# Feed-forward Gelus in two groups of four, with four result slots and later consumers

## The reference

```python
x = x + attention(layernorm(x))
P = layernorm(x) @ U1
H = gelu(P @ V1 + b1, approximate=True)
x = x + (H @ U2) @ V2 + b2
```

## Time and profile before

| what | value |
|---|---|
| runs | 3236.54, 3237.70, 3242.32 us; median 3237.7 us |
| the profiled execution | 3231.01 us; its span 3229.2 us |
| mean granted TensorE clock | 0.972 of full speed |
| busy: PE, DVE, ACT, POOL | 89%, 79%, 75%, 54% of the span |
| Gelus | 128, 81.4 us in all |
| ACT table loads | 61 at the Gelu, 60 at the exponential, 1 at the start |

### The profile page before, as it was taken

The page is one execution under the profiler, slowest core; times in us unless marked ns, Lnnn a source line. Parts: engine busy times, 40 slices in busy tenths (PEclk is TensorE's granted clock), DMA queues, the critical chain, the costliest instruction groups (busy, mean ns, idle before and its releaser), DMA issues.

```text
span 3229.2 us, 98431 instructions
## 1 busy us (share of the span) xinstructions
PE 2884.6 (89%) x32328; PEld 1994.1 (62%) x32328; DVE 2555.6 (79%) x7419; ACT 2422.1 (75%) x4212; POOL 1731.4 (54%) x1560
## 2 busy tenths in 40 slices
PE   4899898998989899898998989989898998989986
PEld 1566565665657666575665656656575665656664
DVE  6888787887878878787787878868788787878863
ACT  3677877777787777787877787777877777777784
POOL 1455555555555555555555555555555555555564
PEclk9999999999999999999999999999999999999998
DMA  4010010100101011010110101001010111101000
GB/s 131 22 34 21 25 33 18 41 20 24 34 18 41 19 30 28 23 36 18 35 26 23 34 17 41 20 24 34 18 42 19 31 26 24 36 16 42 19 19 8
DMA packets 66472, 94.33 MB, mean 29 GB/s; under 512 B 11019, under 2 KB 39691, under 8 KB 65675
## 3 DMA queue, kind: packets, MB, share of 16 engines
q1 hardware_dynamic: 65940, 87.53, 10.9%
HBM read 27.73 MB, written 8.39 MB: 11 GB/s over the span
## 4 chain that ended last, share of the span: by engine, by line
PE 29%; issue 28%; POOL 26%; DVE 6%; ACT 5%; POOLq 1%; DVEq 0%; ACTq 0%
POOL p_lo L1055 24%; PE proj L418 13%; PE scores L418 6%; PE o_acc L418 5%; PE ffn_acc L418 2%; PE max_scores L418 2%; DVE max_scores L902 1%; DVE q_hi_lo L825 1%; ACT L716 1%; ACT h_f L798 1%; DVE v_lo L825 1%; PE transposes L545 1%; ACT p_f L716 1%; ACT L798 1%; POOL h_lo L1078 1%
## 5 line engine op out<-in xcount | busy, mean ns | idle before, releaser
L1055 POOL TENSOR_TENSOR p_lo<-p_f,p_hi 128x512 f16<-128x512 f32 x1280 | 1476.7, 1157 | 1171.7 <-ACT p_hi L674 1140.1
L716 ACT ACTIVATE p_f<-scores 128x512 f32<-128x512 f32 x1280 | 757.7, 592 | 319.5 <-PE scores L418 309.4
L674 ACT ACTIVATE p_hi<-p_f 128x512 f16<-128x512 f32 x1280 | 800.0, 625 | 49.3 <-issue 33.0
L902 DVE CUSTOM_DVE_ANT_0 max_scores<-max_scores,causal 128x384 f32<-128x384 f32 (+3 forms) x1184 | 564.1, 508 | 198.5 <-PE max_scores L418 191.6
L418 PE MATMUL scores<-q_hi_lo,k_lo_hi 128*128 128x512 f16 (+3 forms) x2048 | 622.5, 304 | 28.8 <-issue 27.7
L418 PE MATMUL scores<-q_hi_aug,k_hi_aug 128*128 128x512 f16 (+3 forms) x2048 | 596.7, 304 | 0.0
L418 PE MATMUL o_acc<-v_hi_one,p_lo 128*128 128x65 f16 x5120 | 527.2, 196 | 46.6 <-POOL p_lo L1055 46.5
L418 PEld LDWEIGHTS o_acc<-v_hi_one,p_lo 128*128 128x128 f16 x5120 | 477.1, 99 | 83.7 <-issue 44.8
L418 PE MATMUL o_acc<-v_hi_one,p_hi 128*128 128x65 f16 x5120 | 527.7, 195 | 0.0
L418 PE MATMUL o_acc<-v_lo,p_hi 128*128 128x64 f16 x5120 | 527.5, 194 | 0.0
L418 PEld LDWEIGHTS o_acc<-v_lo,p_hi 128*128 128x128 f16 x5120 | 474.1, 99 | 19.5
(11 more groups left out here) (110 smaller groups left out, 5644.2 us busy)
## 6 DMA issues: line engine op xcount, KB each, us to landing
q_hi_lo<-q_hi_aug SPq DMA_DIRECT2D x256, 128.0 KB, 2.2
k_lo_hi<-k_hi_aug SPq DMA_DIRECT2D x128, 128.0 KB, 2.2
x_rows<-in_L_attn_inputs SPq DMA_DIRECT2D x17, 512.0 KB, 4.5
x_residual<-in_L_attn_inputs SPq DMA_DIRECT2D x16, 512.0 KB, 4.3
out<-x_rows SPq DMA_DIRECT2D x16, 512.0 KB, 4.2
k_hi_aug<-in_k_aug SPq DMA_DIRECT2D x128, 20.0 KB
q_hi_lo<-in_L_attn_W_qkv SPq DMA_DIRECT2D x1, 2048.0 KB, 10.4
q_hi_aug<-in_L_attn_W_qkv SPq DMA_DIRECT2D x1, 2048.0 KB, 15.0
```

The costliest lines, as they stand in the source:

```text
L674: return nc.scalar.activation(out_ap, in_ap, ACT.Copy, scale=scale)
L716: nc.scalar.activation(p_f[:, k % 3, :], score_bank[k % 2][:, :], ACT.Exp).then_inc(exp_done, 1)
L902: last = nc.vector.tensor_tensor_reduce(out=bank, in0=bank, in1=causal[:, (T - 1 - qt) * P:S], scale=1.0, scalar=-3e38, op0=ALU.add, op1=A ...
L1055: nc.gpsimd.tensor_tensor(p_lo[:, slot, n, :], p_f[:, k % 3, :], p_hi[:, slot, n, :], ALU.subtract).then_inc(lo_p, 1)
```

## The change

FFN_PAIRS, until now one table for four engines, is split: FFN_PAIRS is only `ffn_h` on PE, GELU_AT the Gelus on ACT (chunks 0 to 3 at (13, 1), 4 to 7 at (14, 2)), H_PAIRS the cast on DVE and the low part on POOL, U2_PAIRS `ffn_u2` on PE. `h_f32` has four slots instead of two, so Gelu c waits for `h_lo` of chunk c-4 and no more of c-2. `h_hi` and `h_lo` keep two slots. The copy and low part of `ffn_acc` (QF_AT) move from (15, 1) to (15, 2). No operation is added or left out.

```diff
-FFN_PAIRS = {(13, 1): 0, (13, 3): 1, (14, 0): 2, (14, 2): 3}
-
-U2_PAIRS = {(13, 4): 0, (14, 0): 1, (14, 2): 2, (14, 4): 3}
+FFN_PAIRS = {(13, 1): 0, (13, 2): 1, (14, 2): 2, (14, 3): 3}
+
+GELU_AT = {(13, 1): range(0, 4), (14, 2): range(4, 8)}
+
+H_PAIRS = {(13, 2): 0, (13, 4): 1, (14, 3): 2, (15, 0): 3}
+
+U2_PAIRS = {(13, 4): 0, (14, 1): 1, (14, 4): 2, (15, 1): 3}
 U2_START = 13 * SEG + 4
 
-QF_AT, Y_AT = (15, 1), (15, 4)
+QF_AT, Y_AT = (15, 2), (15, 4)
...
-        h_f = sb("h_f32", [P, 2, S], F32)
+        h_f = sb("h_f32", [P, 4, S], F32)
...
-                            if (s, n) in FFN_PAIRS:
-                                for c in (2 * FFN_PAIRS[s, n], 2 * FFN_PAIRS[s, n] + 1):
+                            if (s, n) in GELU_AT:
+                                for c in GELU_AT[s, n]:
                                     act.wait_ge(pe_h, at((i - 1) * FC + c + 1 + FREE))
 
-                                    act.wait_ge(lo_h, at((i - 1) * FC + max(c - 1, 0) + FREE))
-                                    nc.scalar.activation(h_f[:, c % 2, :], proj("h", c)[:, :], ACT.Gelu_apprx_tanh,
+                                    act.wait_ge(lo_h, at((i - 1) * FC + max(c - 3, 0) + FREE))
+                                    nc.scalar.activation(h_f[:, c % 4, :], proj("h", c)[:, :], ACT.Gelu_apprx_tanh,
...
-                            if (s, n) in FFN_PAIRS:
-                                pair = FFN_PAIRS[s, n]
+                            if (s, n) in H_PAIRS:
+                                pair = H_PAIRS[s, n]
...
-                                    nc.vector.tensor_copy(h_hi[:, c % 2, :], h_f[:, c % 2, :]).then_inc(hi_h, 1)
+                                    nc.vector.tensor_copy(h_hi[:, c % 2, :], h_f[:, c % 4, :]).then_inc(hi_h, 1)
...
-                            if (s, n) in FFN_PAIRS:
-                                pair = FFN_PAIRS[s, n]
+                            if (s, n) in H_PAIRS:
+                                pair = H_PAIRS[s, n]
...
-                                    nc.gpsimd.tensor_tensor(h_lo[:, c % 2, :], h_f[:, c % 2, :], h_hi[:, c % 2, :],
+                                    nc.gpsimd.tensor_tensor(h_lo[:, c % 2, :], h_f[:, c % 4, :], h_hi[:, c % 2, :],
```

## The result

The changed kernel takes 3285.9 us (median of four, 3285.09 to 3292.24), the kernel before, run beside it, 3237.1: ratio 1.016, interval 1.014 to 1.018. It is slower by 1.6%; forecast were 3283 us and slower. Its profiled execution has a span of 3290.4 us against 3229.2, so the two profiles differ by 61 us, 12 more than the medians (the profiled execution before is one of the shorter ones, that after the longest of its four), and a stage by 4.0 us.

What follows compares the result with a forecast made beforehand. No engine full: a chain through four in-order engines, PE nearest to full at 89%. 15 stages x 2.9 us plus 1.9 in LAST gave +45.4, from 3231.0 to 3276.4, plus 6.7 to the median: 3283 us, range 3200 to 3312.

Steps and rivals of the forecast that it cites:

- The loads: ACT, MID stages: 4 loads fewer a stage, 5.13 us each stage, 77 us over 15; 31 at Gelu, 30 at exponential.
- The first group: Gelus 0 to 3 at (13, 1): ACT idles 0.97 before Gelu 2; exponential (13, 2) comes 2.1 us later.
- Attend (14, 1): PE at (14, 1): attend waits 1.35 us for POOL's last p_lo, as casts and POOL ops take turns.
- The 1.5 us at the maxima of (14, 0): PE, ahead of attend (14, 1): a wait of 1.5 us for the maxima of (14, 0).
- The second group: Gelus 4 to 7 at (14, 2): h_lo 4 and 5 behind p_lo; PE idles 3.0 at (14, 4), scores (15, 0) +1.55.
- The third piece: (15, 0) to (15, 3): h_lo 6 and 7 end late, ffn_u2 at (15, 1) waits another 0.9; exponential (15, 3) +3.1.
- The signatures: Profile signs: PE's wait for h_lo up to 60 or so, Gelus' wait some 2.5 a stage, maxima waits above 80.8.
- LAST: Final stage: chunk 4's matmuls stand behind ffn_u2 of chunk 3, +1.9 us, and no load saved.
- The clock: PE's granted clock after new idle spells: cost between 0 and +26 us (1.75 a stage), taken as 0.
- B: Rival: ACT is the pace, -2.5 us a stage, to 3202; needs four PE waits under 4.75 us; chance 0.20.
- C: Rival: loads count in full, 77 less 1.9, to 3163; needs Gelus 2 and 6 without a wait; chance 0.04.
- D: Rival, whole kernel: gain and stalls cancel within 0.2%; chance 0.10.

Runs made afterwards that it cites:

- e4: Kernel before with Tanh in place of Gelu, so no table load is left between it and the exponential: 3176.1 us, ratio 0.981.
- e3: Changed kernel with cast and h_lo of chunks 0 and 1 at (13, 1) instead of (13, 2): 3253.3 us, ratio 1.005 to the kernel before.
- e2: Changed kernel with cast and h_lo of chunks 4 and 5 at (14, 2) instead of (14, 3): 3271.6 us, ratio 1.011 to the kernel before.
- e8: Changed kernel with casts, h_lo, ffn_u2 and ffn_acc copy earlier, and matmuls of chunks 6 and 7 at (14, 2), not (14, 3): 3197.9 us, ratio 0.988.
- e9: e8 with the matmuls of chunks 2 and 3 also moved, to (13, 1) ahead of attend instead of (13, 2): 3218.7 us, ratio 0.993.
- e7: Changed kernel with casts, h_lo and ffn_u2 earlier, but the copy of ffn_acc kept at (15, 2): 3223.8 us, ratio 0.996.

## Why the prediction was right

- **The loads.** 31 and 30 as said, at 1.28 each. Taking away all eight loads of a stage gave some 60 us of their 154 (e4). The Trainium skill ("ScalarE: Activation LUTs", What ACT_TABLE_LOAD costs) has 2.66 us for a switch, drain included, which would make them 319, an estimate from that page; the traces show no drain, and the measured number decides.
- **The first group.** The copy, load and exponential behind four Gelus came 2.85 us later on average, 2.1 walked. The stages are of two kinds. In seven of 14, the one shown among them, (13, 2) follows (13, 1) by 7.1 us, just as walked. In the other seven it takes 8.5 to 8.7: TensorE's granted clock was 0.55 to 0.65 in the 2 us from 2 us behind (13, 1) on, PE reached chunk 2 later, and Gelu 2 waited 2.0 to 2.3 instead of 0.9. The very stage that was walked before is now of this second kind:

```profile
1537.60 1.50 ACT L802 ACTIVATE h_f<-proj,b_cols 128x512 f32<-128x512 f32 x2 [2.14 <-PE proj L422]
```

  The first casts came 10.3 us after exponential (13, 1) in the stage shown (1743.08), "some 10". PE waited 2.10 at the maxima of (13, 4), walked 2.4. e3 confirms what that was worth.
- **The wrong terms in it.** Attend (14, 1) waited 0.31 us in the stage shown and 0.66 on average, not 1.35. I had let casts and POOL ops take turns. In the trace the two casts of chunks 2 and 3 took 2.57 us, and POOL ran its two ops beside them in 2.45, all but undelayed:

```profile
1746.09 2.57 DVE L1007 CAST h_hi<-h_f 128x512 f16<-128x512 f32 x2
```

```profile
1745.93 2.45 POOL L1059 TENSOR_TENSOR p_lo<-p_f,p_hi 128x512 f16<-128x512 f32 x2
```

  The 1.5 us at the maxima of (14, 0) were not seen as a wait either. The granted clock was 0.61 there, after 3 us in which PE was busy for 2.02, so the slower matmuls filled them. Attend had to wait for POOL behind them all the same, so this low clock was hidden in a wait, as supposed.

```profile
1747.00:1750.50 3.50, 3.50 (x17) 2.13 (x16) 3.02 (x5) 2.37 (x5) 3.50 (x4) 0.61 0.00 0
```

  In stages of the first kind exponential (14, 2) stands at 21.8, in those of the second at 23.2 to 23.3. The walked 22.7 meets their mean, 22.6, and none of them: the wait of attend was put too high and the wait of Gelu 2 too low, and that they cancel is luck.
- **The second group**, called decisive. POOL's order p_lo, `h_lo` 4, `h_lo` 5 behind the eighth Gelu is there to the letter; PE waited 1.83 + 0.51 + 0.25 = 2.6 us, walked 3.0; exponential (15, 0) was 1.6 us late, walked 1.55. But e2 shows that it is not decisive alone: taken away, it gives 14 us, and the first casts (e3) 33. The step that I called decisive was one of several, and not the largest.
- **The third piece**, from exponential (15, 0) to (15, 3), where `h_lo` 6 and 7 and `ffn_u2` stand at (15, 0) and (15, 1). It grew by 1.7 us a stage (9.4 against 7.7), walked 1.55. No run takes it out alone.
- **The signatures.** PE's wait for `h_lo`, "60 or so", was 51.6. The Gelus' wait for PE, 2.5 us a stage forecast, was 3.1 in the 14 stages, by those of the second kind. PE's wait for maxima should have risen above 80.8 and fell to 73.8; the waits for `h_lo` took their place. LAST grew by 1.8 us (25.1 us from the first Gelu's load to the end against 23.3), walked 1.9.
- **The clock**, taken as 0 with 26 as bound. By the mean it was right, 0.973 after and 0.972 before. But it moved. The 4 us from PE's first scores of a stage on were at a granted clock of 0.59 to 0.67 in 11 of 14 stages, in the kernel before in 2 of 14. One stretch of either sort after the change:

```profile
1782.92:1786.92 4.00, 4.00 (x17) 2.10 (x18) 2.32 (x7) 2.23 (x4) 1.76 (x2) 0.62 0.32 111
2584.58:2588.58 4.00, 4.00 (x47) 2.67 (x48) 2.23 (x7) 2.75 (x5) 2.32 (x2) 1.00 0.40 137
```

  From these scores to exponential (1, 0) the two sorts take 12.9 and 11.2 us, so one costs 1.7, the 1.75 that the forecast had as its bound. Nine more of them are most of the 1.15 us a stage at (0, 1) and (0, 2) that the walk did not have. The 0.70 that rows 8 and 9 lost before and no longer lose offsets more than half of it. The forecast had 45 us against 61 in the profile, 1.1 a stage: 0.66 of it lies ahead of (0, 0), where 3.56 stand against 2.9, and 0.45 is what is left of the clock. Against the medians it was 45 to 49; there is one profile of each kernel, so how often their other executions met the low clock is not known.
- **The rivals.** B (ACT is the pace) had its point of decision: the PE waits at four places under 4.75 us. They were 2.10 + 0.31 + 2.6 + 0.5 = 5.5 in the stage shown, not 7.65 and yet over it. What B took for granted, that saved loads count in full on ACT, e4 measured at 39%. C needed Gelus 2 and 6 without a wait, and they waited 1.5 us each on average. D needed a change within 0.2%.

## What to carry to other kernels

A group of calls saves its table loads only as far as the engine was waited for (here 39% of their time), while every engine that consumes the results in program order has to be placed anew. Walk the in-order queues of the consumers: ask what each new place now stands behind, above all on the slow one. Here the same two groups were 1.6% slower or 1.2% faster than pairs, by the places of casts, low parts, matmuls and one copy alone. When a wait at the end of a chain looks decisive, move the piece ahead of it in one run before believing it, since a second chain may end just behind. And walk more than one stage: here the clock made two kinds of them, 1.5 us apart, and a walk of one stage can only meet their mean by luck.

## What the runs showed of the hardware

- A DVE cast that falls on POOL ops grows from 0.43 to about 1.3 us (2.57 for two), while POOL goes on at 1.2 us an op (2.45 for two, 2.26 without casts). The Trainium skill ("SBUF — State Buffer", Who interferes with whom) says of GpSimd and a VectorE instruction in a 2-port mode, which a cast can enter, that whoever comes second is fully blocked for the other's whole instruction; the trace agrees in that the cast waits, and shows beside it that POOL's next op was held up by 0.1 us at most, not by a whole cast.
- Where TensorE's clock fell decided what it cost. Where matmuls filled the low stretch, from the first scores of a stage on, it cost 1.7 us each time (12.9 against 11.2 us up to exponential (1, 0)); hidden in a wait for POOL, at (14, 0), it cost nothing up to attend (14, 1). Two kernels that differ only in where the matmuls of chunks 2 and 3 stand (e8, e9) met it at the first scores in 3 and in 13 of 14 stages, and their medians differ by 21 us.
- The idle time just ahead does not tell alone whether it falls: e7 had 2.3 to 3.0 us of it ahead of the first scores and kept the full clock behind it in 12 of 14 stages, e9 had 1.9 to 2.4 us and lost it in 13.
